# Attention and feed-forward block: score groups in rounds of two, and one place for both halves of the q stack

## The chip, the cores and the metric

One core of a Trainium2 chip runs the whole program. The metric is the device time in microseconds (us); before the change it is 1669.28 us, the median of three runs (1665.27 to 1671.85). TensorE does the matrix products (PE in the profile, with PEld for its weight loads), ScalarE the activations (ACT), VectorE most elementwise work (DVE), GpSimd some small powers (POOL), and SyncE issues every DMA (SP).

## What is computed

The input is x, 8 batches of 1024 tokens of 256 values. Each batch is layer-normed, and the sum of three things is returned: x, an attention block without softmax, and a feed-forward block with ternary weights. Cut to what matters:

```python
x = L0_attn_x                                    # (8, 1024, 256)
xn = _layernorm(x)
# attention: 16 heads of 16 values
u, v, q, k = split(silu(xn @ W1 + b1), 4)
scores = einsum('bqhd,bkhd->bhqk', q, k)         # 1024 x 1024 a head
attn = silu(scores) / S
av = einsum('bhqk,bkhd->bqhd', attn, v)
y = layernorm(av * u, gamma, beta) @ W2 + b2
# feed-forward: 256 -> 1024 -> 256, weights ternary
h = gelu(layer_norm(xn, ln1_g, ln1_b) @ ternary(w1).T + b1)
out = layer_norm(h, ln2_g, ln2_b) @ ternary(w2).T + b2
return x + y + out
```

## The kernel before, in words

Every engine has a body that it runs once for each of the 8 batches: the first and the last are written out, and the six between are one hardware loop (`Fori(1, NB - 1)`), so the engines jump back five times.

**Groups.** A body has 64 groups. A group is one tile of 128 keys against one half of the queries (512) for four heads. TensorE computes its scores with four matmuls (`scores`, L902), two at a time on the two halves of the array's rows; ScalarE takes the four banks of scores through Silu in two halves of two banks (`silu_group`, L538) into the tile `attn`; TensorE then multiplies them by V (`times_v`, L921: eight recorded matmuls, four at a time on the four column strips of the array). There is one set of four score banks, so each half of a group's scores waits for the Silu of the same half of the group before. Groups 0 to 31 take the first eight heads (c = 0) and groups 32 to 63 the others (c = 1); in each, 16 groups take query half h = 0 and 16 take h = 1.

**Pieces.** All other work of a batch is cut into pieces: `u`, `q`, `k`, `v` are parts of the first projection, `xn` and `xt` norm and transpose the next batch's input, `f1`, `gelu`, `ln2`, `nrm2`, `g` and `f2` are the feed-forward block, `y` makes its input, and `zs`, `zt`, `a` finish the attention of the batch before. The string `TABLE` says which pieces stand behind which group; every engine walks the same table and does its own share of each piece. 68 of them have a TensorE part ("fills"), which goes into one of two PSUM banks `fill` in turn; VectorE or ScalarE empties the bank, and the fill after the next waits for that. Pieces of the next batch (`xn`, `xt`, `v`, `k.0`, `q.0`) run late in a body, those of the last batch (`zs`, `zt`, `a`) early in the following one.

**Order in a group.** TensorE does scores of group g, the fills of row g of the table, then attn x V of group g - 1. ScalarE does the two Silus of group g, then its part of the pieces.

**Stacks of q and k.** The projected k and q are split in a high and a low part, written to DRAM (`write_parts`) and read back as rows for the score matmuls (`load_stack`): KS and QS have a place for both halves of the heads. SyncE issues for each (c, h) six loads of KS and four of QS, and TensorE waits for all ten at the first group that needs one of them: groups 0 and 4 for c = 0, groups 32 and 36 for c = 1.

Of the kernel before, what the change touches and what calls it, by code (L numbers as in the profile page):

```python
# [6 lines left out]
F32 = mybir.dt.float32  # L7
# [6 lines left out]
P = 128  # L14
# [23 lines left out]
STACKED = 16 * 10  # L38
# [20 lines left out]
    "zs.0 zt.0 zs.1 zt.1",  # L59
    "a.0 zs.2",  # L60
    "a.1",
    "zt.2",
    "zs.3 zt.3",
    "a.2",
    "vs.1 a.3 u.1.0 k.1.0 y.0",
    "q.1.0",
    "u.1.1",
    "k.1.1",
    "u.0.1 px q.1.1 u.0.0 y.2",
    "f1.0.0",  # L70
    "f1.0.1",
    "y.1",
    "",
    "f1.1.0 f1.1.1 y.3 gelu.0",
    "f1.2.0 f1.2.1",
    "ln2.0",
    "nrm2.0",
    "f1.3.0 g.0.0",
    "g.0.1",
    "f1.3.1 f2.0",  # L80
    "g.1.0",
    "g.1.1 gelu.1 f1.4.0 f1.4.1",
    "ln2.1 f2.1 f1.5.0",
    "nrm2.1 f1.5.1",
    "g.2.0",
    "g.2.1",
    "f2.2",
    "g.3.0",
    "",
    "",  # L90
    "g.3.1 f1.6.0 gelu.2",
    "f2.3 f1.6.1 f1.7.0",
    "ln2.2 f1.7.1",
    "",
    "",
    "nrm2.2 ln1",
    "",
    "g.4.0",
    "g.4.1 xn.0",
    "f2.4 g.5.0 g.5.1 gelu.3 xt.0",  # L100
    "f2.5 xn.1",
    "xt.1",
    "ln2.3",
    "nrm2.3",
    "k.0.0",
    "g.6.0 xn.2",
    "g.6.1",
    "q.0.0",
    "f2.6",
    "g.7.0",  # L110
    "g.7.1",
    "xt.2",
    "xn.3 v.0",
    "v.1 xt.3",
    "",
    "",
    "",
    "f2.7",
    "k.0.1",
    "q.0.1",  # L120
    "v.2",
    "v.3 vs.0",
# [42 lines left out]

assert not {("zs", 2), ("zs", 3)} & set(SLOTS[0])
# [29 lines left out]
def hybrid_block_kernel(nc, x, W1, b1, b1c, W2, b2, gamc, betc, l1gc, l1bc, w1T, fb1, l2gc, l2bc, w2T, fb2, out):  # L196
# [6 lines left out]
    with ctx:  # L203
# [12 lines left out]
        qs_at = top[0]  # L216
        QS = sb("QS", [P, PAIRS, SEQ], F32R)
# [6 lines left out]
        attn = sb("attn", [P, 2, 4, HALF], F32)  # L224
# [62 lines left out]
        wfraw = at("wfraw", [P, DC, HID], F32, qs_at + 4 * PPC * SEQ)  # L287
        wsraw = at("wsraw", [P, HC, D], F32, qs_at + 4 * PPC * SEQ + 4 * DC * HID)
# [43 lines left out]
        s_stack = [[sem(f"stacked{c}_{h}") for h in range(NH)] for c in range(DC)]  # L332
# [47 lines left out]
        def _(sp):  # L380
# [3 lines left out]
            def write_parts(b, c, h):  # L384

                if c == 0 and h == 0:

                    for cc in range(DC):
                        for hh in range(NH):
                            sp.wait_ge(s_stack[cc][hh], STACKED * b)  # L390
# [716 lines left out]
```

## Time and profile before

| | |
|---|---|
| median of 3 runs | 1669.28 us |
| time of the profiled execution | 1665.21 us |
| its span, first to last instruction | 1663.4 us |
| TensorE busy | 1542.5 us, 93% |
| ScalarE busy | 1226.5 us, 74% (Silu of the scores: 985.3) |
| VectorE busy | 896.1 us, 54% |
| DMA, the main queue | 32.2% of 16 engines' time; all queues 74 GB/s |
| mean granted TensorE clock | 0.982 |

TensorE's busy time counts a matmul from its start to its modelled end, and the ends of pipelined matmuls overlap the next starts. So the page tells that TensorE is nearly always occupied, and the distance between starts tells what a piece of work costs.

### The profile page before, as it was taken

The numbers are of one execution on the slowest core, as the hardware profiler recorded it, in microseconds if no ns is written. First come the engines' busy times: TensorE is split into PE (matmuls) and PEld (weight loads), VectorE is DVE, ScalarE is ACT, GpSimd is POOL, SyncE is SP. The second block draws the span as 40 slices with busy tenths as digits, with TensorE's granted clock in tenths as the row PEclk, the third lists the DMA queues.
The fourth block names the chain that finished last, engine by engine and source line by source line (L and its number), as shares of the span: only waits on it lengthen the run. The fifth ranks groups of instructions, "written<-read, shape, count | busy, mean of one in ns | idle before, by whom it ended". The sixth has DMA issues, their size and how long they took to land.

```text
span 1663.4 us, 27784 instructions
## 1 busy us (share of the span) xinstructions
PE 1542.5 (93%) x9826; PEld 760.8 (46%) x9826; DVE 896.1 (54%) x1716; ACT 1226.5 (74%) x1285; POOL 98.6 (6%) x193
## 2 busy tenths in 40 slices
PE   4799999999899998999989999799997999999997
PEld 3345445444454444444444444444444454544443
DVE  5365735666257553576435664366634657346553
ACT  2378877788668886778857797587875788767884
POOL 2000100000000100001000010000100001000000
PEclk9799999999999999999999999999999999999999
DMA  6470044601544034430335203361034700346000
GB/s 192 90 151 27 6 88 115 123 26 38 110 99 87 26 68 87 127 77 1 77 90 134 57 1 77 90 152 39 1 79 101 152 26 13 88 103 127 1 1 26
DMA packets 62330, 123.68 MB, mean 74 GB/s; under 512 B 7664, under 2 KB 9328, under 8 KB 61168
## 3 DMA queue, kind: packets, MB, share of 16 engines
q1 hardware_dynamic: 62192, 121.81, 32.2%
q8 instruction: 90, 1.47, 0.4%
q14 instruction: 48, 0.39, 0.1%
HBM read 79.84 MB, written 41.94 MB: 73 GB/s over the span
## 4 chain that ended last, share of the span: by engine, by line
issue 75%; PE 15%; POOLq 4%; ACT 3%; DMA 1%; DVE 1%; POOL 1%; SPq 0%; DVEq 0%; ACTq 0%
PE outs L921 5%; PE scores L902 4%; ACT attn L538 2%; POOLq L505 2%; PE fill L992 2%; PE fill L976 1%; PE fill L958 1%; PE fill L985 1%; POOLq L497 1%; POOL rs L491 1%; POOLq L481 1%; DMA QS<-q_scratch 1%; PE fill L1008 0%; DMA q_scratch<-qst 0%; PE fill L967 0%
## 5 line engine op out<-in xcount | busy, mean ns | idle before, releaser
L538 ACT ACTIVATE attn<-scores 128x1024 f32<-128x1024 f32 x1024 | 985.3, 1025 | 361.3 <-PE scores L902 360.9
L921 PE MATMUL outs<-attn,V 128*32 128x512 f32 x4096 | 550.9, 610 | 0.3 <-ACT attn L538 0.3
L902 PE MATMUL scores<-QS,KS 64*128 64x512 f32 x2048 | 414.9, 467 | 57.4 <-ACT attn L538 28.6
L902 PEld LDWEIGHTS scores<-QS,KS 64*128 64x128 f32 x2048 | 172.6, 186 | 533.8 <-ACT attn L538 391.7
L796 DVE TENSOR_TENSOR tmp<-fill,l2g 128x512 f32<-128x512 f32 x128 | 88.5, 691 | 129.6 <-PE fill L985 125.9
L921 PEld LDWEIGHTS outs<-attn,V 128*32 128x32 f32 x4096 | 81.2, 109 | 129.8 <-issue 118.3
L992 PE MATMUL fill<-Wq,hgh 128*128 128x256 f32 x512 | 131.5, 295 | 0.6 <-DVE tmp L796 0.5
L958 PE MATMUL fill<-xp,W1h 128*128 128x512 f32 x384 | 127.9, 415 | 3.0 <-DVE xp L820 3.0
L779 DVE SCALAR_TENSOR_TENSOR hid<-fill,ratq,fb1b 128x512 f32<-128x512 f32 x128 | 96.1, 751 | 61.5 <-PE fill L976 50.8
L992 PE MATMUL fill<-Wq,hgl 128*128 128x256 f32 x512 | 125.2, 282 | 0.0
L992 PEld LDWEIGHTS fill<-Wq,hgh 128*128 128x128 f32 x512 | 97.2, 190 | 18.9 <-issue 16.7
L807 DVE SCALAR_TENSOR_TENSOR part<-fill,cq,part 128x256 f32<-128x256 f32 x64 | 31.0, 484 | 136.2 <-PE fill L992 135.1
L480 POOL TENSOR_TENSOR rp<-mv,epst 128x2 f32<-128x2 f32 x64 | 12.5, 195 | 1500.5 <-DVE mv L700 961.8
L992 PEld LDWEIGHTS fill<-Wq,hgl 128*128 128x128 f32 x512 | 97.4, 190 | 0.3
L803 DVE TENSOR_TENSOR hgl<-tmp,hgh 128x512 fp32r<-128x512 f32 x128 | 88.6, 692 | 9.9 <-issue 0.4
L985 PE MATMUL fill<-ident,hid 128*128 128x128 f32 x512 | 83.4, 285 | 2.9 <-DVE hid L791 1.8
L696 DVE BATCH_NORM_STATS2 st<-hid 128x6 f32<-128x512 f32 x128 | 79.1, 681 | 10.6 <-issue 5.6
L958 PEld LDWEIGHTS fill<-xp,W1h 128*128 128x128 f32 x384 | 67.4, 190 | 35.2 <-issue 22.5
L958 PE MATMUL fill<-xp,W1l 128*128 128x512 f32 x192 | 75.7, 394 | 0.0
L985 PEld LDWEIGHTS fill<-ident,hid 128*128 128x128 f32 x512 | 54.1, 141 | 40.1 <-issue 37.0
L976 PE MATMUL fill<-Wq,yX 128*128 128x512 f32 x256 | 72.2, 413 | 0.0
L976 PE MATMUL fill<-Wq,yT 128*128 128x512 f32 x256 | 71.2, 410 | 0.0
(110 smaller groups left out, 1383.2 us busy)
## 6 DMA issues: line engine op xcount, KB each, us to landing
QS<-q_scratch SPq DMA_DIRECT2D x128, 256.0 KB, 7.2
k_scratch<-kst SPq DMA_DIRECT2D x64, 256.0 KB
q_scratch<-qst SPq DMA_DIRECT2D x64, 256.0 KB
KS<-k_scratch SPq DMA_DIRECT2D x64, 256.0 KB, 4.9
KS<-k_scratch SPq DMA_DIRECT2D x128, 128.0 KB, 5.7
xin<-in_x SPq DMA_DIRECT2D x8, 1024.0 KB, 4.8
out_dram<-part SPq DMA_DIRECT2D x16, 512.0 KB, 2.7
w1raw<-in_W SPq DMA_DIRECT2D x1, 1024.0 KB, 7.1
```

Of the source, the lines that this page charges most:

```text
L505: pool.drain()
L538: nc.scalar.activation(attn[:, g % 2, 2 * hf:2 * hf + 2, :], SP[:, 2 * hf:2 * hf + 2, :], ACT.Silu).then_inc(s_silu, 1)
L696: V_.bn_stats(st[:, j, n, :] if len(views) > 1 else st[:, j, :], v)
L779: V_.scalar_tensor_tensor(out=hid_of(t)[:, cols], in0=FP[:, k, :], scalar=ratq[:, t:t + 1], in1=fb1b[:, cols], op0=ALU.mult, op1=ALU.add). ...
L796: V_.tensor_tensor(tmp[:, :].rearrange("p (c n) -> p c n", n=P), FP[:, k, :].rearrange("p (c n) -> p c n", n=P), l2g[:, 4 * r:4 * r + 4].u ...
L803: V_.tensor_tensor(hgl[:, r, :], tmp[:, :], hgh[:, r, :].bitcast(F32), ALU.subtract).then_inc(s_hg, 1)
L902: ins = mm(SP[:, j, :], KS[rows, pair, t * P:(t + 1) * P], QS[rows, pair, h * HALF:(h + 1) * HALF], start=True, stop=True)
L921: ins = mm(OP[32 * j:32 * j + 32, g // RUN % 2, :], V[:, t, c * HPC // 2 + j, o * DH:o * DH + 2 * DH], attn[:, g % 2, n, :], start=(o == 0 ...
L958: ins = mm(bank.rearrange("p (i n) -> p i n", i=2), w[:, kc, col:col + P], xp[:, 2 * h:2 * h + 2, part, kc, :], start=n == 0, stop=n == le ...
L976: ins = mm(bank, y_of(t // 2)[:, part, kc, t % 2 * P:(t % 2 + 1) * P], Wq1[:, kc, hf * HALF:(hf + 1) * HALF], start=n == 0, stop=n == len( ...
L985: ins = nc.tensor.transpose(bank[:, n * P:(n + 1) * P], hid_of(t)[:, col:col + P], ident[:, :])
L992: ins = mm(bank[:, 0:D], w[:, r, n * P:(n + 1) * P], Wq2[:, 4 * r + n, :], start=i == 0, stop=i == len(passes) - 1)
```

## The change

Two groups now share a round. TensorE does the scores of group 2n, attn x V of groups 2n - 2 and 2n - 1, the scores of group 2n + 1, then the pieces of both rows of the table. ScalarE does four Silu halves, then the pieces of both rows. `attn` has three buffers in place of two. The table is another one: the same pieces in other rows. QS holds one half of the heads; k and q have semaphores of their own, the loads of QS are issued behind those of KS, and each half h of QS is loaded when the last score group that reads the old content is done. TensorE waits for QS at the first group of each run of 16, and for KS where it waited for both.

```diff
 TABLE = (
-    "zs.0 zt.0 zs.1 zt.1",
-    "a.0 zs.2",
...
+    "zt.0 zs.0 zt.1",
+    "zs.1",
+    "a.0 zs.2 zt.2",
...
-        QS = sb("QS", [P, PAIRS, SEQ], F32R)
+        QS = sb("QS", [P, PPC, SEQ], F32R)
...
-        attn = sb("attn", [P, 2, 4, HALF], F32)
+        attn = sb("attn", [P, 3, 4, HALF], F32)
...
+        def attn_of(g):
+            return attn[:, 2 if g % 2 else g // 2 % 2, :, :]
...
-            def load_stack(b, c, h, reused):
-                if reused and h == 0:
-                    sp.wait_ge(s_score, 2 * GROUPS * (b - 1) + 2 * PHASE * (c + 1))
+            def load_k(b, c, h):
                 written = 4 * WROTE * b + WROTE * (NH * c + h + 1)
                 sp.wait_ge(s_kw, written)
                 sp.wait_ge(s_qw, written)
...
+            def load_q(b, c, h, reused):
+                if reused:
+                    user = GROUPS * b if c else GROUPS * (b - 1) + PHASE
+                    sp.wait_ge(s_score, 2 * (user + RUN * (h + 1)))
...
                 for h in range(NH):
-                    write_parts(b, 1, h)
+                    write_parts(b, 1, h, not first)
                     if first and h == 0:
                         sp.wait_ge(s_tern, 2)
-                    load_stack(b, 1, h, not first)
+                    load_k(b, 1, h)
+                for h in range(NH):
+                    load_q(b, 1, h, True)
                 if not last:
                     wait_evacuated(sp, b, ("f1", T - 3, 1))
                     load_x(b + 1)
                     for h in range(NH):
-                        write_parts(b + 1, 0, h)
-                        load_stack(b + 1, 0, h, True)
+                        write_parts(b + 1, 0, h, True)
+                        load_k(b + 1, 0, h)
+                        load_q(b + 1, 0, h, True)
...
 # ScalarE
-                for g in range(GROUPS):
-                    silu_group(b, g, first)
-                    for s in steps(g, first, last):
-                        step(b, first, *s)
+                for n in range(SLOTS2):
+                    for g in (2 * n, 2 * n + 1):
+                        silu_group(b, g, first)
+                    for g in (2 * n, 2 * n + 1):
+                        for s in steps(g, first, last):
+                            step(b, first, *s)
...
 # VectorE
+                for n in range(SLOTS2):
+                    if n == 0 and not first:
                         output(b - 1, DC * NH - 1)
-                    if g and g % RUN == 0:
-                        output(b, g // RUN - 1)
+                    elif n and 2 * n % RUN == 0:
+                        output(b, 2 * n // RUN - 1)
...
 # TensorE
                 if g % PHASE in (0, T // 2):
-                    pe.wait_ge(s_stack[c][g % PHASE // (T // 2)], STACKED * (b + 1))
+                    pe.wait_ge(s_kst[c][g % PHASE // (T // 2)], K_STACKED * (b + 1))
+                if g % RUN == 0:
+                    pe.wait_ge(s_qst[h], Q_STACKED * (DC * b + c + 1))
...
-                for g in range(GROUPS):
-                    scores(b, g, first)
-                    if g == 0 and not first:
-                        times_v(b - 1, GROUPS - 1, False)
-                    if first:
-                        setup_step(g)
-                    for s in steps(g, first, last):
-                        step(b, *s)
-                    if g:
-                        times_v(b, g - 1, first)
+                for n in range(SLOTS2):
+                    scores(b, 2 * n, first)
+                    for g in (2 * n - 2, 2 * n - 1):
+                        if n:
+                            times_v(b, g, first)
+                        elif not first:
+                            times_v(b - 1, GROUPS + g, False)
+                    scores(b, 2 * n + 1, first)
+                    for g in (2 * n, 2 * n + 1):
+                        if first:
+                            setup_step(g)
+                        for s in steps(g, first, last):
+                            step(b, *s)
```

TensorE in the first body before, behind the fill of table row 34 (`f1.7.1`, L976), where groups without a fill follow (L921 is attn x V, L902 the scores):

```order
L976 MATMUL fill<-Wq,yT 128x512 x4
L921 MATMUL outs<-attn,V 32x512 x4
L902 MATMUL scores<-QS,KS 128x512 x4
L921 MATMUL outs<-attn,V 32x512 x4
L902 MATMUL scores<-QS,KS 128x512 x4
```

and rounds 17 to 19 of the changed kernel, which also begin behind one `f1` fill (L994; L939 is attn x V, L920 the scores):

```order
L994 MATMUL fill<-Wq,yT 128x512 x4
L920 MATMUL scores<-QS,KS 128x512 x4
L939 MATMUL outs<-attn,V 32x512 x8
L920 MATMUL scores<-QS,KS 128x512 x8
L939 MATMUL outs<-attn,V 32x512 x8
```

Two attn x V now stand together, so do two scores where a round has no fill, and a fill is followed by scores and no longer by attn x V.

SyncE at the end of a body before, the parts and the stacks of (c, h) = (0, 1) of the next batch:

```order
L396 DMA k_scratch<-kst 8x16x512 x2
L399 DMA q_scratch<-qst 8x16x512 x2
L416 DMA KS<-k_scratch 32x4x512
L416 DMA KS<-k_scratch 16x4x512 x2
L419 DMA QS<-q_scratch 32x4x512 x2
L416 DMA KS<-k_scratch 32x4x512
L416 DMA KS<-k_scratch 16x4x512 x2
L419 DMA QS<-q_scratch 32x4x512 x2
```

and in the changed kernel:

```order
L399 DMA k_scratch<-kst 8x16x512 x2
L402 DMA q_scratch<-qst 8x16x512 x2
L414 DMA KS<-k_scratch 32x4x512
L414 DMA KS<-k_scratch 16x4x512 x2
L414 DMA KS<-k_scratch 32x4x512
L414 DMA KS<-k_scratch 16x4x512 x2
L427 DMA QS<-q_scratch 32x4x512 x4
```

All six loads of KS now stand ahead of the four of QS.

VectorE at the head of the loop body before, the first rows behind the branch:

```order
L741 CAST yT<-uz 128x512
L743 TENSOR_TENSOR yT<-uz,yT 128x512
L348 ISA
L732 BN_STATS st_96<-fill 128x6 x2
L736 BN_AGGR mv_97<-st_96 128x2 x2
```

and in the changed kernel:

```order
L352 ISA
L734 SCALAR_TENSOR_TENSOR uz<-outs,uz 128x512
L349 ISA
L746 BN_STATS st_96<-fill 128x6 x2
L750 BN_AGGR mv_97<-st_96 128x2 x2
L755 CAST yT<-uz 128x512
L757 TENSOR_TENSOR yT<-uz,yT 128x512
```

The product of the last attention output with u (L734, before L720) has moved to the front, and the split `zs.0`, on which the first `a` waits, has moved behind the moments of `zt.0`.

## Rows read from the trace of the kernel before

**Rows 1.** Windows of the first loop body, all six, and the last body: span, busy times.
```profile
252.08:448.17 196.09, 188.79 (x1229) 92.84 (x1225) 109.69 (x210) 153.54 (x162) 11.46 (x23) 1.00 0.34 77
252.08:1456.55 1204.47, 1141.33 (x7348) 562.21 (x7344) 658.04 (x1260) 915.80 (x961) 68.77 (x138) 0.99 0.33 74
1456.55:1641.22 184.67, 176.40 (x1129) 81.90 (x1126) 93.16 (x170) 145.29 (x150) 7.13 (x16) 0.98 0.25 52
```

**Rows 2.** Timeline of TensorE, steady stretch: start, length, line, operation, count.
```profile
403.47 0.73 PE L958 MATMUL fill<-xp,W1h 128*128 128x512 f32 x2
...
405.06 1.06 PE L921 MATMUL outs<-attn,V 128*32 128x512 f32 x8
406.06 0.73 PE L902 MATMUL scores<-QS,KS 64*128 64x512 f32 x4
406.72 0.39 PE L992 MATMUL fill<-Wq,hgh 128*128 128x256 f32 x1
...
408.49 0.28 PE L992 MATMUL fill<-Wq,hgh 128*128 128x256 f32 x1
408.61 0.28 PE L992 MATMUL fill<-Wq,hgl 128*128 128x256 f32 x1
408.82 1.07 PE L921 MATMUL outs<-attn,V 128*32 128x512 f32 x8
...
410.48 0.65 PE L985 MATMUL fill<-ident,hid 128*128 128x128 f32 x4
411.06 1.07 PE L921 MATMUL outs<-attn,V 128*32 128x512 f32 x8
```

**Rows 3.** Timeline of TensorE, the second four of the eight at 405.06 alone.
```profile
405.52 0.61 PE L921 MATMUL outs<-attn,V 128*32 128x512 f32 x4
```

**Rows 4.** Timeline of TensorE, one `f1` fill, and a group without a fill.
```profile
494.48 1.20 PE L976 MATMUL fill<-Wq,yT 128*128 128x512 f32 x4
495.61 1.07 PE L921 MATMUL outs<-attn,V 128*32 128x512 f32 x8
...
501.05 0.50 PE L902 MATMUL scores<-QS,KS 64*128 64x512 f32 x2
501.92 0.50 PE L902 MATMUL scores<-QS,KS 64*128 64x512 f32 x2 [0.38 <-ACT attn L538]
...
503.35 0.91 PE L902 MATMUL scores<-QS,KS 64*128 64x512 f32 x4
```

**Rows 5.** Timeline of ScalarE: Silu behind the scores of 448.17, and around a Gelu.
```profile
448.71 1.94 ACT L538 ACTIVATE attn<-scores 128x1024 f32<-128x1024 f32 x2 [0.90 <-PE scores L902]
...
505.86 1.28 ACT L582 ACT_TABLE_LOAD   x1
...
510.38 1.94 ACT L538 ACTIVATE attn<-scores 128x1024 f32<-128x1024 f32 x2
```

**Rows 6.** Timeline of TensorE where the loop jumps back, and group 4 of the last body.
```profile
448.17 0.73 PE L902 MATMUL scores<-QS,KS 64*128 64x512 f32 x4 [1.35 <-issue]
...
449.83 1.09 PE L1002 MATMUL fill<-ident,uz 128*128 128x128 f32 x8
450.85 0.73 PE L902 MATMUL scores<-QS,KS 64*128 64x512 f32 x4
453.50 0.50 PE L1008 MATMUL fill<-W2h,yT 128*128 128x256 f32 x2 [1.92 <-DVE st L732]
...
1471.30 1.22 PE L902 MATMUL scores<-QS,KS 64*128 64x512 f32 x4 [3.16 <-DMA QS<-q_scratch]
```

**Rows 7.** Timeline of VectorE behind the same jump.
```profile
451.23 0.43 DVE L741 CAST yT<-uz 128x512 fp32r<-128x512 f32 x1 [4.68 <-issue]
...
457.66 0.25 DVE L736 BATCH_NORM_AGGREGATE mv<-st 128x2 f32<-128x6 f32 x2 [4.30 <-issue]
```

**Rows 8.** Timeline of SyncE: parts of q written, then stacks read.
```profile
441.26 1.20 SPq L399 DMA_DIRECT2D q_scratch<-qst  x2
446.61 1.25 SPq L416 DMA_DIRECT2D KS<-k_scratch  x3
```

More of the change, by code:

```diff
@@ L37 @@
 WROTE = 16 * PARTS
-STACKED = 16 * 10
+K_STACKED = 16 * 6
+Q_STACKED = 16 * 4
+SLOTS2 = GROUPS // 2
 TABLE = (
-    "zs.0 zt.0 zs.1 zt.1",
-    "a.0 zs.2",
[L61 to L88, printed above, removed]
-    "",
-    "",
-    "g.3.1 f1.6.0 gelu.2",
-    "f2.3 f1.6.1 f1.7.0",
-    "ln2.2 f1.7.1",
-    "",
-    "",
-    "nrm2.2 ln1",
-    "",
[L98 to L106, printed above, removed]
+    "zt.0 zs.0 zt.1",
+    "zs.1",
+    "a.0 zs.2 zt.2",
+    "",
+    "",
+    "a.1 a.2 zs.3 zt.3",
+    "a.3 u.1.0",
+    "",
+    "k.1.0 px q.1.0",
+    "u.0.0 u.1.1",
+    "",
+    "y.1 k.1.1 y.0 q.1.1",
+    "u.0.1 f1.0.0 y.2",
+    "",
+    "",
+    "f1.0.1 f1.1.0 f1.1.1 y.3 gelu.0 f1.2.0 ln2.0 f1.2.1",
+    "nrm2.0",
+    "f1.3.0",
+    "f1.3.1",
+    "",
+    "g.0.0 g.0.1",
+    "",
+    "f2.0 g.1.0",
+    "g.1.1 gelu.1 f1.4.0",
+    "ln2.1 f2.1",
+    "",
+    "",
+    "nrm2.1 g.2.0 g.2.1",
+    "",
+    "vs.1 f2.2 g.3.0",
+    "f1.4.1",
+    "g.3.1",
+    "f1.5.0 f1.5.1",
+    "f1.6.0 gelu.2 ln2.2 f2.3",
+    "",
+    "ln1 f1.6.1",
+    "",
+    "",
+    "xn.0",
+    "nrm2.2 g.4.0 g.4.1",
+    "",
+    "f1.7.0 f1.7.1 f2.4 g.5.0 g.5.1 gelu.3 ln2.3",
+    "xt.0",
+    "xn.1 f2.5",
+    "nrm2.3 v.0 xt.1",
+    "",
+    "xn.2 g.6.0",
     "g.6.1",
+    "",
+    "f2.6",
+    "k.0.0 g.7.0",
+    "",
     "q.0.0",
-    "f2.6",
-    "g.7.0",
     "g.7.1",
     "xt.2",
-    "xn.3 v.0",
-    "v.1 xt.3",
-    "",
-    "",
+    "v.1",
+    "xn.3 v.2",
+    "xt.3",
+    "",
+    "v.3",
+    "k.0.1 q.0.1",
     "",
     "f2.7",
[L119 to L122, printed above, removed]
+    "vs.0",
 )
@@ L331, in hybrid_block_kernel @@
         s_qw = sem("q_parts_written")
-        s_stack = [[sem(f"stacked{c}_{h}") for h in range(NH)] for c in range(DC)]
+        s_kst = [[sem(f"k_stacked{c}_{h}") for h in range(NH)] for c in range(DC)]
+        s_qst = [sem(f"q_stacked{h}") for h in range(NH)]
         s_v = sem("v_ready")
@@ L382, in load_x, with write_parts @@
                 sp.dma_start(xin[:, :, :], xv[b, :, :, :]).then_inc(s_x, 16)
[L384 to L390, printed above, removed]
+            def write_parts(b, c, h, reused):
+                if reused and h == 0:
+                    sp.wait_ge(s_score, 2 * GROUPS * (b - 1) + 2 * PHASE * (c + 1))
                 cols = slice(h * HALF, (h + 1) * HALF)
@@ L901, in scores @@
                     pair = c * PPC + j // 2 * 2 + o
[L902 removed]
+                    ins = mm(SP[:, j, :], KS[rows, pair, t * P:(t + 1) * P], QS[rows, pair - c * PPC, h * HALF:(h + 1) * HALF],
                              start=True, stop=True)
@@ L921, in times_v @@
                     ins = mm(OP[32 * j:32 * j + 32, g // RUN % 2, :], V[:, t, c * HPC // 2 + j, o * DH:o * DH + 2 * DH],
-                             attn[:, g % 2, n, :], start=(o == 0 and t == 0), stop=(o == 1 and t == T - 1))
+                             attn_of(g)[:, n, :], start=(o == 0 and t == 0), stop=(o == 1 and t == T - 1))
                 ins.then_inc(s_av, 1)
@@ L1039, in body @@
             def body(b, first=False, last=False):
-                for g in range(GROUPS):
-                    scores(b, g, first)
-                    if g == 0 and not first:
-                        times_v(b - 1, GROUPS - 1, False)
-                    if first:
-                        setup_step(g)
-                    for s in steps(g, first, last):
-                        step(b, *s)
-                    if g:
-                        times_v(b, g - 1, first)
+                for n in range(SLOTS2):
[6 more added lines that the diff above has]
+                    scores(b, 2 * n + 1, first)
+                    for g in (2 * n, 2 * n + 1):
+                        if first:
+                            setup_step(g)
+                        for s in steps(g, first, last):
+                            step(b, *s)
             pe.wait_ge(s_ident, 1)
@@ L1064, in _ @@
             body(NB - 1, last=True)
-            times_v(NB - 1, GROUPS - 1, False, last=True)
+            for g in (GROUPS - 2, GROUPS - 1):
+                times_v(NB - 1, g, False, last=True)
             for s in EPI:
```

25 lines of the change are left out of this document (13 added, 12 removed).

## The prediction

> **What bounds the kernel now.** I read the windows of whole bodies first. One body takes 196.1 us, the six loop bodies together 1204.5, so 201.7 for the five that are entered by a jump; in them TensorE is occupied for 94% and more, ScalarE for 76%, VectorE for 55% [rows 1]. TensorE is the engine to count, and since its modelled ends overlap, I count from start to start. The timeline of a steady stretch gives the prices, always up to the start of what follows:
> - scores of a group: 406.72 - 406.06 = 0.66; attn x V: 406.06 - 405.06 = 1.00, of which the first four take 0.46 and the last four 0.54 [rows 2, 3]. A group without fill costs 1.66.
> - fills: `u`, `k`, `q` 405.06 - 403.47 = 1.59; `f2` 408.82 - 406.72 = 2.10; `g` 0.58, and `zt`, `xt` alike (four transposes) [rows 2]; `f1` 1.13 [rows 4]. `a` and `v` have 12 matmuls of the width of the 16 of `f2`: estimate 1.60.
> - two kinds of seam: inside `f2` the starts are 0.12 apart, the last matmul before attn x V takes 0.21, so 0.09 is lost at the seam; and attn x V loses 0.54 - 0.46 = 0.08 to 0.09 before scores [rows 2, 3].
>
> Sum of a body: 64 x 1.66 = 106.2, fills 12 x 1.59 + 16 x 1.13 + 8 x 2.10 + 24 x 0.58 + 8 x 1.60 = 80.7, less 0.09 for each of the 19 fills that follow another fill of their group (68 fills stand in 49 groups): 185.2. The first loop body takes 196.1, so TensorE waits 10.9 there: 1.4 at the jump back (1.35 of it shown for the next jump [rows 6]), 2.0 at group 4 for the stacks (3.16 in the last body [rows 6]), and 7.5 in the middle. Those are of one kind: in two groups without fill ScalarE, which needs 1.94 for two halves [rows 5], cannot keep up, and the second takes 503.35 - 501.05 = 2.30 in place of 1.66 [rows 4]; a little is due to Gelu. The bodies behind a jump lose 5 to 6 more than this one: VectorE stands for 4.68 and again for 4.30 us for nothing but the next instruction [rows 7], `a.0` waits for it (1.92 [rows 6]), and `a.1` more.
>
> **The order changed.** The same matmuls are issued. A round is scores 0.66, first attn x V 0.46 + 0.46 = 0.91 (no seam), second 1.00, scores 0.66: 3.23 in place of 3.32. Fills now end before scores and not before attn x V: unseen in a steady stretch, but at the jump two `zt` lead into scores, and take 450.85 - 449.83 = 1.02 for eight transposes [rows 6], 0.51 each, less than 0.58; I take the same seam of 0.09. The fills of a body now stand in 31 rounds, so 37 of them follow another: 32 x 3.23 + 80.7 - 37 x 0.09 = 180.7. The seams give 4.5 a body.
>
> **Waits of a round.** A Silu starts 448.71 - 448.17 = 0.54 behind its scores, and both halves are done 1.94 later [rows 5]. The second half of scores 2n + 1 wants the Silu of 2n at 0.66 + 1.91 + 0.34 = 2.91 from the round's start and has it at 2.48: no wait, 0.43 to spare. The second half of scores 2n + 2 wants the Silu of 2n + 1 at 1.00 + P behind the start of scores 2n + 1, and has it at 2.53, where P is the fills' time. So a round with P under 1.53 waits for the rest. Nine rounds are so short: 0, 8, 9, 10, 13, 17, 19 and 23 with two `g`, two `zt` or one `f1`, P 1.07 to 1.13 (0.40 to 0.46 each), and round 18 without a fill (1.53): 5.0 in all, less 0.7 where a Gelu has already made TensorE late: 4.3.
>
> Gelu holds ScalarE from 505.86 to 510.38 with both table loads, 4.52 [rows 5]. In round 11 (`f2.0 g.1.0 g.1.1 f1.4.0`, P 4.1 and some 0.7 for banks that VectorE has yet to empty) it follows the Silu at 2.48 behind scores 23 and ends at 7.0; scores 24 start at 5.5, scores 25 want Silu 24 at 8.1 and 8.4, and have it at 8.0 and 8.9: 0.55 lost. Where Gelu waits for the evacuation of an `f1`, its first table load stands before the wait: the same count gives 0.3 in rounds 16 and 20, and 1.15 in round 7. Sum 2.3. VectorE does some 1.9 for a `g`, and two `g` now stand in one round: three places where a fill wants a bank 0.3 too early, 1.0 with small ones. So the middle of a body keeps 7.6 of waits, as many as before: what the pairs win in groups without a fill goes to short rounds and Gelu.
>
> **The stacks at the start of a body.** TensorE wants KS of (0, 1) at group 4, before as now, but k.0.1 and q.0.1 have moved to round 30. Before, in the last body, all ten loads were in place 22.3 us behind the end of the q fill (group 61; 1449.0, by 3.27 + 3.28 for two groups and 1.00 back from 1456.55). Now group 4 follows 15.4 behind it (round 31 5.3, round 0 4.8, round 1 5.3). Bound above: if all ten were still needed, 6.9 would be lost where no jump stands between (two bodies) and up to 5 elsewhere. Bound below: nothing. Only six loads count, half the bytes: 2.06 to the split, 446.61 - 441.26 = 5.35 until the parts are written [rows 8], six issues in 2.9 and 5.7 to land (an estimate from the share of bytes): 16.0. I take 0.6 in two bodies, 1.2 in all. QS of the half that is overwritten is wanted 16 groups after it is free, some 50 us: hidden. The loads of x are issued behind `f1.5.1` and land before `ln1` has its turn: hidden, by some 1 to 2 us only.
>
> **The jump.** It stays, 1.5 for TensorE. VectorE's rows at the loop's head are as many as before, so both gaps stay. It now branches 0.9 later against the first scores (`f2.7` is last), so it resumes about 3.8 behind them and the second gap ends at 10 to 11.5 (before 9.5 [rows 6, 7]); then comes `zs.0`, 1.2, and `a.0` can start near 11.7. TensorE wants it at 8.0, behind round 0 and the two scores and products of round 1. So 3.7 lost, and 1.0 for matmuls at the lower clock behind such a gap: 4.7. Bounds: 0 if the gaps are covered, and 7.6, what they cost now: 201.7 - 196.1, and the 2.0 at group 4 that only the first body has.
>
> The Trainium skill ("Runtime: NRT & Kernel Launch", Instruction fetch mechanics) says that a taken branch forces a fetch of the target page and stalls, while the crossing into the next 16 KiB block is mostly hidden. The trace agrees on the first gap, 4.68, and not on the second, 4.30 [rows 7]. By the page only the first would be left, `a.0` would be ready at about 7, and the time would be that of rival A.
>
> **The sum.** First loop body: 180.7 + 4.3 + 2.3 + 1.0 + 1.5 = 189.8. Four bodies with jumps on both sides 194.5, the sixth 193.0. Together 1160.8 against 1204.5: -43.7. Last body: many pieces are gone (`k.0`, `q.0`, `v`, `xt`), so that the sum without waits is 166.3 and short rounds come to 14.6; with the same 0.7, 2.3 and 1.0 that is 183.5, and with 1.9 for the last two products 185.4, against 184.67 and one group's 1.66 plus 0.6 of waiting: -1.5. First body: its set-up is bound by VectorE and transfers, its other groups gain 2.8, the start 1. Prologue: `v.0` now stands before `xt.1` and the first `k`: +1.2. Stacks +1.2. In all -46.6 on the profiled execution's 1665.2: 1618.6. The median of before stands 4.1 above its profiled execution: **1623 us**.
>
> **Rivals.**
> - A: the fetch gaps no longer reach TensorE (VectorE asks before the loads of KS saturate the DMA engines). For: loads are issued later against the branch. Against: the second gap came in each of the five jumps. 5 x 4.7 less: 1599.
> - B: the 0.43 to spare isn't there. In some 16 rounds ScalarE still projects the last fill when the next scores are ready, or a bank is late; 0.35 lost in each is 5.6 a body, 45 in all: 1667. For: the margin is one short delay wide. Against: a projection ends 0.9 behind its fill, the Silu could start at 0.54, so 0.36 fits in 0.43.
> - C, slower: Gelu. Two Silu groups and the evacuation of `f1` now stand before it, and a whole round's products behind it; if VectorE is late with that evacuation (`y`, `ln2` and pairs of `g` in the same round), all four Gelu of a body push the next round by 2.0 more than counted: 4 x 2.0 x 8 = 64, 1687. It decides from 46 / 32 = 1.5 each. For: four rounds hold 4 to 8 pieces. Against: ScalarE has 42 us to spare in a body [rows 1], and before, Gelu cost little in the same place.
> That the change isn't made can't be: the order shows it.
>
> **Chances.** Forecast 0.60 (own range 1600 to 1650), A 0.16, B 0.12, C 0.12. A measurement of this kernel tells about 0.5% (8 us) from no change. Faster: forecast, A and a quarter of B, 0.79; same 0.09; slower 0.12. The range reaches below A and up to B: 1590 to 1665.
>
> **What would show it.** Right: a first loop body of about 190 and the others of 193 to 195; attn x V of two groups 1.9 us from start to start of what follows; the wait of round 18 near 1.5; no waits over 1.5 behind a Gelu; `a.0` waiting some 4 us behind each jump and `a.1` not at all; group 4 hardly waiting for KS. Wrong: DVE or ACT as the releaser of fills and scores in most rounds, a body over 200, or a seam between fills and scores dearer than 0.09.

## The result and the profile after

The changed kernel takes 1599.58 us (median of 4 runs, 1597.45 to 1600.69); the kernel before, beside it on the same chip, 1667.28 (1663.10 to 1671.85). The ratio is 0.9592, 95% interval 0.9562 to 0.9622: 67.7 us faster. Forecast were 46 less than before, 1623 with a range of 1590 to 1665. The time lies in the range, and below the forecast's own range of 1600 to 1650; it is the number of rival A.

The page of the changed kernel, span, busy times and the two costliest lines of TensorE (busy us, mean ns of one, idle before):

```profile
span 1595.7 us, 27804 instructions
PE 1482.5 (93%) x9826; PEld 778.7 (49%) x9826; DVE 896.9 (56%) x1716; ACT 1223.6 (77%) x1285; POOL 98.7 (6%) x193
L939 PE MATMUL outs<-attn,V 128*32 128x512 f32 x4096 | 501.0, 607 | 0.0
L920 PE MATMUL scores<-QS,KS 64*128 64x512 f32 x2048 | 407.9, 461 | 74.8 <-ACT attn L550 51.9
```

The matmuls are the same, and TensorE is still 93% busy. Its busy time fell by 60 because overlapping ends are counted: only starts tell where time went. Windows of the first loop body, the five bodies behind a jump, and the last body (span, busy PE, PEld, DVE, ACT, POOL, granted clock, DMA share, GB/s) answer to [rows 1]:

```profile
240.69:435.12 194.43, 184.20 (x1226) 96.40 (x1226) 110.25 (x211) 152.97 (x162) 11.53 (x23) 0.98 0.33 78
435.12:1386.95 951.83, 911.53 (x6120) 478.94 (x6121) 548.36 (x1049) 761.01 (x799) 57.65 (x115) 0.99 0.33 78
1386.95:1568.42 181.47, 165.66 (x1097) 81.26 (x1096) 93.35 (x170) 142.25 (x148) 7.13 (x16) 0.99 0.25 56
```

The third window ends at the scores of group 62, and the third of [rows 1] at those of group 63; these stand at 1571.62 here, 184.67 behind the body's first scores, just as before.

From first scores to first scores of each body, both traces:

| | before | after | change | forecast |
|---|---|---|---|---|
| up to the first scores | 46.50 | 47.93 | +1.4 | +1.2 |
| first body | 205.57 | 192.75 | -12.8 | -3.8 |
| first loop body | 196.09 | 194.43 | -1.7 | -5.7 |
| five bodies behind a jump | 1008.39 | 951.83 | -56.6 | -37.4 |
| last body, to its last matmul | 202.56 | 203.89 | +1.3 | -0.9 |

So the sign was right, and the distribution was not: most of it lies in the bodies behind a jump. Before, such a body took 5.6 more than the first loop body; now it takes 4.1 less (951.83 / 5 = 190.4). Of the 56.6, 32.3 lie between a body's first scores and those of its group 6, and 24.3 in the rest, 4.9 a body; in the first loop body, which no jump delays, that rest gains 4.8, too. TensorE at the first jump of the changed kernel, answering to [rows 6] (start, length, line, operation, count, idle before and its releaser):

```profile
435.12 0.73 PE L920 MATMUL scores<-QS,KS 64*128 64x512 f32 x4 [1.66 <-issue]
435.78 1.93 PE L939 MATMUL outs<-attn,V 128*32 128x512 f32 x16
437.64 0.74 PE L920 MATMUL scores<-QS,KS 64*128 64x512 f32 x4
438.30 1.09 PE L1020 MATMUL fill<-ident,uz 128*128 128x128 f32 x8
439.33 0.50 PE L920 MATMUL scores<-QS,KS 64*128 64x512 f32 x2
...
442.46 0.73 PE L920 MATMUL scores<-QS,KS 64*128 64x512 f32 x4
444.37 0.51 PE L1026 MATMUL fill<-W2h,yT 128*128 128x256 f32 x2 [1.18 <-DVE yT L757]
```

and VectorE behind the same jump, answering to [rows 7]:

```profile
438.98 0.69 DVE L734 SCALAR_TENSOR_TENSOR uz<-outs,uz 128x512 f32<-128x512 f32 x1 [5.00 <-issue]
...
442.81 0.18 DVE L750 BATCH_NORM_AGGREGATE mv<-st 128x2 f32<-128x6 f32 x1 [1.93 <-issue]
```

The first gap is much as before, 5.00, and VectorE resumes 3.9 behind the first scores, as forecast (3.8). The second is 1.93 and not 4.30; in the other four bodies it is 1.95, 0.97, 0.73 and 0.71, where before had 4.38, 6.08, 6.17 and 6.22. It ends 7.7 behind the first scores (forecast: 10 to 11.5). `a.0` waits 1.18 behind the first jump, 0.81 behind the second and not at all behind the others (forecast 3.7, and 1.0 more for slow matmuls). Behind these three, though, TensorE comes late by itself: the first pair of products runs at a granted clock near the lower of the two levels (0.59 over the first round at the fourth jump, where 1 is 2.4 GHz and 0.5 is 1.2 GHz) and takes 3.17 in place of 1.93:

```profile
1006.95 1.10 PE L920 MATMUL scores<-QS,KS 64*128 64x512 f32 x4 [2.14 <-issue]
1007.97 3.17 PE L939 MATMUL outs<-attn,V 128*32 128x512 f32 x16
```

TensorE's waits for what VectorE makes in `zs` and `zt`, in the whole program (us in total, times, longest), before and after; the longest one after, 2.4, stands behind the last body:

```profile
PE fill L1008 <- DVE st L732: 31.7, 13, 5.3
```
```profile
PE fill L1026 <- DVE yT L757: 4.4, 3, 2.4
```

SyncE's stack loads:

```profile
437.65 2.67 SPq L414 DMA_DIRECT2D KS<-k_scratch  x6
```

They now start 2.5 behind the first scores (2.0 to 2.5 over the five jumps). Before, they started 448.17 - 446.61 = 1.6 ahead of them [rows 6, 8] (1.6 to 2.0). That is the suspicion which the experiments below test.

TensorE at group 4 of the first loop body, which no jump delays:

```profile
253.34 1.22 PE L920 MATMUL scores<-QS,KS 64*128 64x512 f32 x4 [2.53 <-DMA KS<-k_scratch]
```

Here the stacks are late, by more than the 0.6 that was taken. In the first body the same place has the opposite sign: 1.30 of waiting, where the kernel before had 6.56.

```profile
61.44 0.73 PE L920 MATMUL scores<-QS,KS 64*128 64x512 f32 x4 [1.30 <-DMA KS<-k_scratch]
```

### The profile page after: what moved, and what is told of

It reads as the page before. It is cut to its first block, busy times and chain, and to the rows that moved or that the text cites. A ratio compares the mean times of both kernels' runs of the same rounds, so it can differ in the third digit from the quotient of the medians.

```text
span 1595.7 us, 27804 instructions
## 1 busy us (share of the span) xinstructions
PE 1482.5 (93%) x9826; PEld 778.7 (49%) x9826; DVE 896.9 (56%) x1716; ACT 1223.6 (77%) x1285; POOL 98.7 (6%) x193
## 4 chain that ended last, share of the span: by engine, by line
issue 93%; POOLq 6%; POOL 1%; DVE 0%; DVEq 0%
POOLq L517 3%; POOLq L509 1%; POOLq L493 1%; POOL rs L503 1%; POOLq L502 0%; POOLq L511 0%; POOLq L507 0%; POOLq L505 0%; POOLq L519 0%; POOLq L522 0%; POOLq L203 0%; POOL rs L494 0%; DVE part L764 0%; DVEq L203 0%; POOLq L536 0%
## 5 line engine op out<-in xcount | busy, mean ns | idle before, releaser
L939 PE MATMUL outs<-attn,V 128*32 128x512 f32 x4096 | 501.0, 607 | 0.0
L920 PE MATMUL scores<-QS,KS 64*128 64x512 f32 x2048 | 407.9, 461 | 74.8 <-ACT attn L550 51.9
L920 PEld LDWEIGHTS scores<-QS,KS 64*128 64x128 f32 x2048 | 165.3, 186 | 390.6 <-ACT attn L550 314.6
L939 PEld LDWEIGHTS outs<-attn,V 128*32 128x32 f32 x4096 | 108.0, 110 | 240.8 <-issue 240.7
L976 PE MATMUL fill<-xp,W1h 128*128 128x512 f32 x384 | 125.5, 408 | 2.3 <-DVE xp L834 1.5
L492 POOL TENSOR_TENSOR rp<-mv,epst 128x2 f32<-128x2 f32 x64 | 12.5, 195 | 1443.6 <-DVE mv L714 884.9
L840 DVE CAST kst<-kst 128x512 fp32r<-128x512 f32 x32 | 13.7, 428 | 133.6 <-ACT kst L556 133.6
L976 PEld LDWEIGHTS fill<-xp,W1h 128*128 128x128 f32 x384 | 68.3, 189 | 30.0 <-issue 15.1
L1003 PE MATMUL fill<-ident,hid 128*128 128x128 f32 x512 | 74.3, 278 | 2.3
L976 PE MATMUL fill<-xp,W1l 128*128 128x512 f32 x192 | 75.4, 393 | 0.0
L994 PE MATMUL fill<-Wq,yX 128*128 128x512 f32 x256 | 72.9, 416 | 1.5 <-DVE tmp L810 1.2
L994 PE MATMUL fill<-Wq,yT 128*128 128x512 f32 x256 | 70.7, 410 | 0.0
```

The costliest lines, as they stand in the source:

```text
L920: ins = mm(SP[:, j, :], KS[rows, pair, t * P:(t + 1) * P], QS[rows, pair - c * PPC, h * HALF:(h + 1) * HALF], start=True, stop=True)
L939: ins = mm(OP[32 * j:32 * j + 32, g // RUN % 2, :], V[:, t, c * HPC // 2 + j, o * DH:o * DH + 2 * DH], attn_of(g)[:, n, :], start=(o == 0 ...
L976: ins = mm(bank.rearrange("p (i n) -> p i n", i=2), w[:, kc, col:col + P], xp[:, 2 * h:2 * h + 2, part, kc, :], start=n == 0, stop=n == le ...
L994: ins = mm(bank, y_of(t // 2)[:, part, kc, t % 2 * P:(t % 2 + 1) * P], Wq1[:, kc, hf * HALF:(hf + 1) * HALF], start=n == 0, stop=n == len( ...
L1003: ins = nc.tensor.transpose(bank[:, n * P:(n + 1) * P], hid_of(t)[:, col:col + P], ident[:, :])
```

## Experiments

They were timed in three comparisons: `b_split`, `a_wait_all`, `a_seams` and `b_newtable` beside a median of 1665.13 for the kernel before, `a_oldtable`, `b_unrolled`, `a_unrolled` and `a_k_early` beside 1663.85, `b_q_later`, `a_unrolled_k` and `a_tail` beside 1669.36. A name with b is an edit of the kernel before, one with a of the changed kernel; ratios are to the kernel before in the same comparison. "To group 6" means from a body's first scores to those of its group 6.

### The split of KS and QS alone, and without it

`b_split`, the kernel before with own semaphores, KS loads ahead of QS, QS awaited at groups 0, 16, 32 and 48:

```diff
 # TensorE's waits; semaphores and order of the loads left out
-pe.wait_ge(s_stack[c][g % PHASE // (T // 2)], STACKED * (b + 1))
+pe.wait_ge(s_kst[c][g % PHASE // (T // 2)], K_STACKED * (b + 1))
+if g % RUN == 0:
+    pe.wait_ge(s_qst[c][h], Q_STACKED * (b + 1))
```

> The kernel before, with its table, its order of groups and both places of QS, but KS and QS have semaphores of their own, the six loads of KS are issued ahead of the four of QS, and TensorE waits for QS only at the first group of each run of 16. Theory (the stacks): the waits at group 4 shrink where no jump hides them: first body 6.6 us to about 1, body 1 2.0 to 0, last body 3.2 to 0, with a little lower-clock time behind them; the bodies behind a jump are bound by VectorE and stay. Sum -10 to -12 us: about 1656 against 1667. Rival (the changed kernel's gain at the start of a body is only that two pairs of scores and products stand before group 4): no difference, 1667.

Measured: 1650.33, ratio 0.9916 (0.9891 to 0.9941), 14.8 less, and a little more than the theory's 10 to 12. First body 199.87 (before 205.57), to group 6 25.61 (before 31.37). The bodies behind a jump stayed at 198.6 to 203.5.

`a_wait_all`, the changed kernel, where TensorE waits for QS as well at groups 4 and 36:

```diff
-if g % RUN == 0:
-    pe.wait_ge(s_qst[h], Q_STACKED * (DC * b + c + 1))
+if g % PHASE in (0, T // 2):
+    pe.wait_ge(s_qst[g % PHASE // (T // 2)], Q_STACKED * (DC * b + c + 1))
```

> The changed kernel, but TensorE waits for the QS loads at group 4 as well (and at 0, 32, 36), as before, in place of at the first group of a run of 16. The loads of QS h = 1 are issued right behind those of KS. Theory (the stacks): ten loads saturate the DMA engines until some 15 us behind the first scores of a body, group 4 stands at 11 to 12: +3 to 4 us in each of the five bodies behind a jump, +4 to 6 in bodies 0, 1 and 7, in all +30 to +40: about 1635. Rival: KS alone is what is late and QS lands with it, at most +5: 1605.

Measured: 1648.88, ratio 0.9895 (0.9843 to 0.9947). Nearly 50 of the 67.7 are gone, more than either theory had. First body 199.89, so 7.1 back; bodies behind jumps 196.1 to 198.1, 7 more each. All of it lies in front of group 6 (in the first of these bodies 25.34 from the first scores, where the changed kernel has 18.00); groups 32 to 40 take as long as in the changed kernel, so the second wait, at group 36, costs nothing. TensorE at group 4 of a jump body of this kernel:

```profile
460.52 1.22 PE L920 MATMUL scores<-QS,KS 64*128 64x512 f32 x4 [4.38 <-DMA QS<-q_scratch]
461.67 3.64 PE L939 MATMUL outs<-attn,V 128*32 128x512 f32 x16
```

A wait of 4.38 is followed by matmuls that take 3.64 where 1.92 is normal: their granted clock is 0.50, the lower level (1.2 GHz). From group 4 to group 8 this body takes 15.39 where the changed kernel takes 12.88, so the wait costs 7 and not 4.4. What follows: the rounds reach group 4 so early that they cannot live with the old wait. The split is worth 15 to the kernel before and some 50 to the changed one (0.9895 against 0.9592). The prediction called the full wait its bound above, at 6.9 where no jump stands between and "up to 5 elsewhere"; elsewhere it is 7 too.

### Rounds and table, each alone

`a_seams`, the changed kernel with scores between the two attn x V, pieces still in rounds, `attn` with four buffers:

```diff
 # one round of TensorE, in short
-scores(2n); times_v(2n-2); times_v(2n-1); scores(2n+1); pieces
+scores(2n); times_v(2n-2); scores(2n+1); times_v(2n-1); pieces
```

> The changed kernel, but in a round TensorE does scores 2n, attn x V of 2n - 2, scores 2n + 1, attn x V of 2n - 1, then the fills (attn has four buffers for it). Theory (two products between the scores cover the Silu): besides the seam of 0.09 in each of 256 rounds (+23 us), the second half of scores 2n + 1 now wants its Silu 2.0 us behind the round's start and has it at 2.5, so a round loses 0.5 more, less what short rounds win back: +14 to 18 a body, 1710 to 1740. Rival (only the seams count, since ScalarE has time to spare): +23, 1623.

Measured: 1723.80, ratio 1.0342 (1.0288 to 1.0396), as the theory had it. Bodies of 206.0 to 213.0. In a round TensorE waits for the Silu of 2n, begun only 0.54 behind its scores, since attn x V of one group is shorter than that Silu:

```profile
1110.52 0.73 PE L920 MATMUL scores<-QS,KS 64*128 64x512 f32 x4
1111.18 1.07 PE L939 MATMUL outs<-attn,V 128*32 128x512 f32 x8
1112.18 0.49 PE L920 MATMUL scores<-QS,KS 64*128 64x512 f32 x2
1113.05 0.50 PE L920 MATMUL scores<-QS,KS 64*128 64x512 f32 x2 [0.38 <-ACT attn L550]
```

From 1112.18 to 1113.05 are 0.87, where two halves in one go are 0.33 apart: 0.54 a round. So the pair of products is what hides the Silu of 2n.

`b_newtable`, the kernel before with the new table:

> The kernel before in all but the table, which is that of the changed kernel, walked group by group. Theory (the round is what makes the bunched table good): fills stand in fewer groups, so more groups without a fill follow each other and wait for ScalarE, 0.2 to 0.6 us each; the middle of a body loses 3 to 6 us, and zs and a, spread wider, win back 3 at the five jumps: 1665 to 1700. Rival (the table alone carries the gain): 1600 to 1625.

Measured: 1727.09, ratio 1.0355 (1.0299 to 1.0412). Slower, as the theory had it, but by 62, where its range ended at 35. TensorE's waits of this kernel (us in total, times, longest):

```profile
PE scores L902 <- ACT attn L538: 88.0, 185, 1.7
PE scores L902 <- DMA QS<-q_scratch: 32.4, 9, 6.6
```

Before, the wait for Silu was 28.6 in 86 places, 59 less, and that for QS 20.2 in 4, 12 less. The second is not the table's alone: this kernel still awaits all ten loads at group 4, and the new table sends them later. The new table with the split but without rounds was not run.

`a_oldtable`, the changed kernel with the old table (the two edits are one literal, quoted in the change):

> The changed kernel with the table of the kernel before; rounds, waits and loads as changed. With b_newtable (the other half alone: 1727) it says whether rounds and table are worth anything apart. Theory (the rounds win by themselves, the table only spreads the pieces for them): 80.7 of fills and the seams as in the changed kernel, but k.0.1 and q.0.1 stand in other rows, a.0 is in round 0 and wants VectorE's split some 2 us before it can be there: five jump bodies lose 2 to 4 more each, and rounds without a fill stand closer together: 1615 to 1640. Rival 1 (the table adds nothing to the rounds): 1600, within 5. Rival 2 (the gain is the table's with the rounds only as its condition): over 1655.

Measured: 1731.64, ratio 1.0409 (1.0362 to 1.0456). Both theory (1615 to 1640) and rival 1 fell; rival 2 is nearer, yet it is not the table's gain either, since the table alone loses 60. TensorE's waits:

```profile
PE scores L920 <- ACT attn L550: 99.6, 170, 2.8
...
PE fill L1026 <- DVE st L746: 21.0, 10, 3.5
PE fill L1003 <- DVE hid L805: 15.6, 8, 2.6
PE fill L994 <- DVE tmp L810: 9.8, 16, 0.9
```

In the changed kernel the first of these rows is 51.9 in 126 places, longest 0.9. Round by round, over the first four loop bodies, rounds 8 to 12, where the first Gelu and `y.3` fall, take 41.9 in place of 29.4, 12.5 of the 16.3 that a body loses. Behind two `f1` with a Gelu the scores wait 2.8, and then a `g` waits 2.0 for VectorE. Rounds and table are one edit: each without the other ends 60 or more above the kernel before (the table without the split, the rounds with it), together with the split of KS and QS they bring 68. That the old table's trouble is the short rounds beside Gelu is read from these rows; no run moved Gelu alone.

### The jump

`b_unrolled` and `a_unrolled`, both kernels with the six loop bodies written out one behind another on all engines:

```diff
 # for each of the five engines, eng standing for it
-with eng.Fori(1, NB - 1) as b:
-    body(b)
+for b in range(1, NB - 1):
+    body(b)
```

> The kernel before with its six loop bodies written out one behind another on every engine: no engine branches back, everything else is the same. Theory (a jump costs TensorE 1.35 itself and 4 to 5 through VectorE's two gaps): five times 5 to 6 less: 1637 to 1642 against 1665. Rival (straight code of six bodies is fetched while it runs, so that gaps of the second kind, 4.3 and more, come in every body wherever the DMA engines are full): 1655 or slower.

Measured: 1628.84, ratio 0.9799 (0.9777 to 0.9820), 35 less, 8 below the theory's range. Five of the six bodies now take 194.1 to 194.9, one 198.3. VectorE's waits of over 1 us for the next instruction are gone. The rival (fetching while straight code runs) fell. What the jumps had hidden comes to light here already: every loop body now waits for the loads at group 4, 1.8 to 2.2 and once, in the body of 198.3, 4.38, where the five bodies behind a jump had no such wait.

> The changed kernel with its six loop bodies written out on every engine. Theory: five times 1.66 (jump) and 1.2 (a.0 behind VectorE's gaps) go: 14 less, 1583 to 1588; and the difference to the unrolled kernel before is 50 to 56, smaller than the 67.7 of the two with jumps: 12 to 18 of the gain came from cheaper jumps. Rival (jumps played no part in the gain): the unrolled kernels lie 66 to 70 apart.

Measured: 1603.32, ratio 0.9640 (0.9623 to 0.9656): not faster than the changed kernel with its jumps, whose ratio is 0.9592. Neither theory nor rival: the two unrolled kernels lie 25.5 apart and not 50 to 56. The trace shows why, in the body that begins at 432.13:

```profile
439.46 0.73 PE L920 MATMUL scores<-QS,KS 64*128 64x512 f32 x4
440.13 0.51 PE L1026 MATMUL fill<-W2h,yT 128*128 128x256 f32 x2
...
444.75 0.73 PE L920 MATMUL scores<-QS,KS 64*128 64x512 f32 x4 [2.49 <-DMA KS<-k_scratch]
```

The jump's 1.66 and the 1.18 of `a.0` are gone, and TensorE waits 2.49 for KS at group 4 instead: eight such waits, 20.0 in all, where the kernel with jumps has three, 6.2. The jumps had been covering the loads. Without jumps the change is worth 25.5. The other 42 of its 67.7 belong to the jumps: 35 that they cost the kernel before, and some 7 that the changed kernel takes less with them than without.

### Loads against VectorE's fetch

`a_k_early`, the changed kernel with the stacks' pieces one round earlier:

```diff
     "",
-    "v.3",
     "k.0.1 q.0.1",
+    "v.3",
     "",
```

> The changed kernel with the row 'k.0.1 q.0.1' one round earlier, in the place of 'v.3', and v.3 in its row. Theory of contention (VectorE's second fetch behind the jump is short, 1.93, only because the KS loads are issued behind the branch and have not yet filled the DMA engines): the bodies with no jump in front (first loop body, last body) lose their wait for KS at group 4 and the slow matmuls behind it, 3 to 4 each; the five others get their loads 4 to 5 us earlier against the branch, so the second gap grows to 3.5 to 4.5 and a.0 waits 2 to 4 instead of 1.2: +1 to +3 each. 1594 to 1606. Rival (the second gap does not depend on the loads, it is the order of VectorE's code): second gap stays near 1.9, a.0 near 1.2, the two bodies win 3 to 4 each: 1591 to 1594.

Measured: 1605.75, ratio 0.9645 (0.9627 to 0.9663), against 0.9592: slower, at the upper end of the theory's range. First loop body 189.16 and no wait for KS (194.43 in the changed kernel). The last body has no such wait either, and is at group 6 after 16.76 in place of 20.81, but it takes 206.70 and not 203.89 in the profiled execution (the slowest of the four, 1612.29): several of its later rounds run at the lower clock. The five bodies behind a jump take 15 more together. The loads now start 2.2 to 3.0 ahead of the first scores, and VectorE's second gap is 3.35, 1.58, 5.43, 4.31 and 4.03. `a.0` waits for it, in the third of them:

```profile
828.78 0.18 DVE L750 BATCH_NORM_AGGREGATE mv<-st 128x2 f32<-128x6 f32 x1 [5.43 <-issue]
```
```profile
830.34 0.80 PE L1026 MATMUL fill<-W2h,yT 128*128 128x256 f32 x2 [4.90 <-DVE yT L757]
```

`b_q_later`, the converse, in the kernel before: `q.0.1` one group later, so that the loads start 1.7 to 2.2 behind the first scores. VectorE's code at the jump is untouched.

```diff
     "k.0.1",
-    "q.0.1",
     "v.2",
+    "q.0.1",
```

> The kernel before with q.0.1 and v.2 exchanged in the table, so that the parts of (0, 1) are complete one group later and SyncE issues the stack loads some 1.5 behind the first scores of the next body, as in the changed kernel, and not 1.6 to 2.0 ahead of them. Nothing in VectorE's code at the jump moves. Theory (VectorE's second fetch is slow because the loads already fill the DMA engines): the second gap falls from 4.3 to 6.2 to 3 or less in the five jump bodies; group 4, which wants all ten loads, waits for them instead, so the time need not fall: 1655 to 1670. Rival (the gap belongs to the place in VectorE's code): second gap 4.3 to 6.2 as before in all five.

Measured: 1656.54, ratio 0.9927 (0.9904 to 0.9950). One exchange of two rows is worth 13 us (8 to 16). In the traces the five bodies behind a jump gain 15.4, and the first loop body and the last one lose 7.8, since they now wait 5.31 and 6.03 at group 4. VectorE behind the first jump:

```profile
456.01 0.43 DVE L741 CAST yT<-uz 128x512 fp32r<-128x512 f32 x1 [5.11 <-issue]
...
460.08 0.25 DVE L736 BATCH_NORM_AGGREGATE mv<-st 128x2 f32<-128x6 f32 x2 [1.94 <-issue]
```

The second gap is 1.94, 2.07, 2.00, 2.02 and 2.04 in the five bodies, and was 4.30 to 6.22. The rival that it belongs to the place in the code is out. The DMA view of the kernel before, of the 0.1 us from 454.80, shows a packet of the instruction queue:

```profile
q1 hardware_dynamic: 9, 0.02, 95.5%
q14 instruction: 1, 0.01, 55.4%
```

It starts 3.6 behind the instruction at 451.23 that ended the first gap. In the changed kernel the like packet is found in the 0.1 us from 440.35, 1.4 behind 438.98:

```profile
q1 hardware_dynamic: 7, 0.01, 104.2%
q14 instruction: 1, 0.01, 35.4%
```

In this experiment it also starts 1.4 behind (457.46), and in the third jump of the one before, 5.2 behind. VectorE goes on 1.6 to 2.0 after each of these packets has ended. That it is VectorE's fetch is read from its timing; the trace doesn't name an engine, and has the start of a packet, not when it was asked for.

All nine kernels with jumps tell the same. Take, behind each of the five jumps, the first two packets of the instruction queue from 3 us ahead of the first scores on. In six kernels (the changed one, `a_wait_all`, `a_seams`, `a_oldtable`, `b_newtable`, `b_q_later`) the KS loads start 0.7 behind the first of the two, and the second starts 3.1 to 3.8 behind the first. In the other three (the one before, `b_split`, `a_k_early`) the loads start 0.9 to 3.5 ahead of the first, and the second comes 5.4 to 8.3 behind it. `b_newtable` is the telling one: its loads start 0.3 to 0.7 ahead of the first scores and still behind that packet, and its second gaps are short, 0.9 to 1.4. So it is the place of the loads against the fetch that counts, not against the scores, and the simplest reading is that the second packet waits for its turn among the loads' packets.

### Together

`a_unrolled_k`, the changed kernel with both edits that had lost alone.

> The changed kernel with its loop bodies written out and 'k.0.1 q.0.1' one round earlier: both edits that lost time alone (1603 and 1606) together. Theory: written out, no fetch gap is left that earlier loads could lengthen, and the wait for KS at group 4 (8 times, 20.0 in all in a_unrolled) goes with the slow matmuls behind it, 3.5 to 4 in each of seven or eight bodies: 1571 to 1580. Rival (DMA loads beside the head of a body cost something else, or group 4 then waits for the next thing): 1590 or more.

Measured: 1572.83 (1571.40 to 1574.88), ratio 0.9417 (0.9397 to 0.9438). TensorE waits for KS once in the whole program (2.3, in the first body), and a body takes 187.05; the windows of one:

```profile
427.62:614.64 187.02, 181.16 (x1225) 95.74 (x1224) 109.68 (x210) 152.37 (x161) 11.56 (x23) 1.00 0.33 80
```

`a_tail`, the same with scores between the products in the last rounds of the last body, which have hardly any fill:

```diff
+if last and n >= 26 and g % 2 == 0:
+    scores(b, 2 * n + 1, first)
...
-scores(b, 2 * n + 1, first)
+if not (last and n >= 26):
+    scores(b, 2 * n + 1, first)
```

> a_unrolled_k, and in rounds 26 to 31 of the last body, which have no or hardly any fill, the scores of group 2n+1 stand between the two attn x V (attn has four buffers). In a_seams such a round took 3.96, in the changed kernel 4.81, because scores 2n+1 then wait for no Silu that began only behind scores 2n. Theory: 4 x 0.85 and some 0.3 for round 26: 3.5 to 4 less than a_unrolled_k. Rival (the end is bound by ScalarE's last Silus anyway): no difference.

Measured: 1571.73 (1569.56 to 1572.55), ratio 0.9409 (0.9388 to 0.9430). The rounds went from 4.81 to 3.96 as expected, and the last body from 203.48 to 196.33; of these 7.2, 3.3 are two rounds that in the kernel above ran at the lower clock, and here don't. But in the profiled run three other bodies took some 1.7 more each, behind matmuls at the lower clock in other places, and the runs' times overlap those of the kernel above. Whether it is faster isn't settled. Both beat both kernels: 97 and 98 us below the one before.

## Why the prediction was right or wrong

**Right: the rounds themselves.** The pair of products was to take 1.91 from start to start of scores and takes 437.64 - 435.78 = 1.86. The round without a fill was to wait 1.53; it waits 0.95 ahead of its first half (361.03, due 0.66 behind the scores of 359.41) and 0.58 ahead of the second (0.91 from start to start in place of 0.33). Round 18 of the first loop body of the changed kernel:

```profile
361.03 0.50 PE L920 MATMUL scores<-QS,KS 64*128 64x512 f32 x2 [0.89 <-ACT attn L550]
361.94 0.49 PE L920 MATMUL scores<-QS,KS 64*128 64x512 f32 x2 [0.41 <-ACT attn L550]
```

The body without jump and stack waits was to take 189.8 - 1.5 = 188.3; the last experiments have it bare, 187.05. Rival B (the 0.43 to spare isn't there) is out: `a_k_early`'s first loop body, with one jump at its end, takes 189.16 against the forecast's 189.8. Rival C is out: no scores wait over 0.9 for Silu behind a Gelu (51.9 in 126 places, longest 0.9). That margin exists in this table only; in the old one such waits reach 2.8.

**Wrong: the step "so it resumes about 3.8 behind them and the second gap ends at 10 to 11.5".** The first half held. The second took the gap of before, 4.30, for a property of VectorE's rows, though the loads had moved against it. Measured: it ends at 7.2 to 7.7. Of the 4.7 for each of five bodies, 1.2 are left in the first and 0.8 in the second as a wait of `a.0`, and 1.6 in each of the others, there as the pair of products at the lower clock, behind which `a.0` is ready in time. So the lower clock was rightly expected, but behind the jump itself and not behind `a.0`. Why it comes behind three jumps and not behind two is open: TensorE's gaps there are 1.86 to 2.15 against 1.66 and 1.86. The prediction had the order's rows for SyncE and counted 16.0 until the stacks are there, but did not carry the loads' start over to the jump. That is rival A, by its own mechanism, and the two tests with moved loads show it. By the rule of the Trainium skill that stood beside it ("Runtime: NRT & Kernel Launch", Instruction fetch mechanics: a crossing into the next block is mostly hidden) the number was right, too; yet the runs show no rule that always holds: in straight code nothing over 0.5 is seen, at a jump 0.7 to 2.1, and up to 6.2 beside loads that had started. The chance of 0.16 was too small: "the second gap came in each of the five jumps" was one fact, since the loads stood at the same place five times.

**Wrong in size: the stacks at group 4.** Taken was 0.6 in two bodies. The wait is 2.53 in the first loop body and 2.40 in the last, and with the slow matmuls behind it the first loop body is 194.43 - 189.16 = 5.3 longer than with earlier loads. The need was right: TensorE asks at 253.34 - 2.53 = 250.81, 15.4 behind the end of the q fill at 235.40, as forecast. The loads were late at one term: k and q now stand in one row, their four part writes come together, and from the q parts' issue to the KS loads pass 7.2 and not 5.35 [rows 8]:

```profile
236.14 1.20 SPq L399 DMA_DIRECT2D k_scratch<-kst  x2
237.51 1.90 SPq L402 DMA_DIRECT2D q_scratch<-qst  x2
244.75 2.67 SPq L414 DMA_DIRECT2D KS<-k_scratch  x6
```

**Missed: the first body.** "The start 1" was 5.7 from the split alone (shown by the first experiment) and 7.1 with the rounds (the second): its group 4 had waited 6.56 for all ten loads, and I had read that wait only in the last body [rows 6]. The kernel before:

```profile
64.72 1.22 PE L902 MATMUL scores<-QS,KS 64*128 64x512 f32 x4 [6.56 <-DMA QS<-q_scratch]
```

The body's other 5.7, where 2.8 were counted, were not followed up.

**A number right by cancelling.** Rival A's 1599 lacked the first body's further 9.0. Against that it had 6.2 too little in the first loop body and the last one (4.0 and 2.2 by the table) and 4.3 too little in the five bodies behind a jump (-37.4 - 23.5 against -56.6). Its mechanism is shown; that it fits to 1 us is chance.

**Not asked: what a jump hides.** The prediction asked what the loads cost where no jump stands in front, and what a jump costs, but not that the second hides the first. In both unrolled kernels the wait at group 4 comes up in every body.

**Right, and a loss: the end.** The last body gained nothing, as the count of short rounds had it. Its four rounds without a fill take 4.81 each (counted: 3.23 + 1.53), where two such groups took 3.96 to 4.13, since the Silu of the round's second group starts only behind its late scores; `a_tail`, with 3.96, shows that the order does it.

## What to carry to other kernels

A gap whose cause is a transfer belongs to the time at which other transfers run, not to the engine's code: when an edit moves loads, move them in the timeline against every such gap before pricing it. An order of work and the table that spreads the rest over it are one edit, and must be tried together. A delay taken away shows what it had covered, so two edits that each lose alone can win together.

## What the runs showed of the hardware

- Instruction fetch beside loads: VectorE's second gap behind a jump is 0.7 to 2.1 where the loads start 1.7 to 2.5 behind the first scores (changed kernel, `b_q_later`), and 1.6 to 6.2 where they start 1.6 to 3.0 ahead (kernel before, `b_split`, `a_k_early`). The DMA engines are full in the short gaps too (share 1.05 from 440.88 to 442.81), so the share alone doesn't tell the two apart. Where in the queue the fetch waits isn't shown.
- At a jump back TensorE stands 1.35 to 2.2 for the next instruction, and VectorE 3.2 to 5.4 (first gap). Written out, the same bodies show no wait for the next instruction over 0.5 on VectorE.
- What TensorE's clock adds to a wait: behind the waits of 2.53 and 4.38 the pair of products took 3.64 in place of 1.92, at the lower granted level, and the body was 5.3 and 7 longer. At three of the changed kernel's jumps it took 3.17 to 3.20, behind gaps of 1.86 to 2.15. In `a_tail`, `a_unrolled_k` and `a_k_early`, single rounds ran 1.6 longer at that level behind no wait of such a length; what set those off is open.
